# A graph kernel: the transposes of the adjacency matrix move from the attention scores into the first pass over reversed edges

## The reference, cut to what matters

```
x = layernorm(x + gcn3(x))            # three sums over incoming edges
x = layernorm(x + gat(x))             # per edge: a score from x_l[src], x_r[dst], weight; softmax by dst
x = layernorm(x + sage2(x))           # two sums over incoming edges
# the last layer sums over the REVERSED edges: out of a node, not into it
agg  = segment_sum(x[dst], src)       # row, col = src, dst
h    = relu(agg  / deg_out @ W1.T + b1)
agg2 = segment_sum(h[dst], src)
x = layernorm(x + relu(agg2 / deg_out @ W2.T + b2))
```

## Time and profile before

| | |
|---|---|
| median of three runs | 5697.41 us (5667.19 to 5700.05) |
| the profiled execution | 5702.34 us, of which its span is 5700.5 us |
| TensorE matmul busy | 3324.1 us, 58% |
| VectorE busy | 2808.7 us, 49% |
| ScalarE busy | 1675.3 us, 29% |
| GpSimd busy | 2048.7 us, 36% |
| scores stage | about 2350 to 3626 us |
| first back pass, strips | about 4954 to 5285 us |
| second back pass, strips | about 5308 to 5644 us |

### The profile page before, as it was taken

One profiled execution on the slowest core, in us unless ns is written; L12 is line 12 of the kernel. 1 busy time (PEld: TensorE's weight loads), 2 busy tenths in 40 slices (PEclk: granted clock), 3 DMA queues, 4 the chain that ended last, 5 costly groups with the idle time before them and its releaser, 6 DMA issues.

```text
span 5700.5 us, 61044 instructions
## 1 busy us (share of the span) xinstructions
PE 3324.1 (58%) x19159; PEld 3100.7 (54%) x19160; DVE 2808.7 (49%) x3801; ACT 1675.3 (29%) x2774; POOL 2048.7 (36%) x1982
## 2 busy tenths in 40 slices
PE   1300000019999999544444444357479999689697
PEld 0300000019999999544333343246379789589597
DVE  8300000024454544677666677788954344544345
ACT  0000000005645455200000000023266356456265
POOL 2777666750000000377677777346300000200300
PEclk9999999999999999755555555579789999799798
DMA  9700000008858587499899899247368268478585
GB/s 356 275 1 16 1 1 1 1 12 278 257 183 276 175 275 227 126 228 220 215 216 214 215 221 222 62 122 214 92 205 277 84 208 277 151 244 285 180 283 183
DMA packets 887483, 1008.44 MB, mean 177 GB/s; under 512 B 391651, under 2 KB 651705, under 8 KB 887270
## 3 DMA queue, kind: packets, MB, share of 16 engines
q1 hardware_dynamic: 795778, 861.50, 51.6%
q0 software_dynamic: 56208, 63.97, 4.8%
q10 hardware_dynamic: 35284, 80.30, 3.6%
HBM read 692.09 MB, written 233.14 MB: 162 GB/s over the span
## 4 chain that ended last, share of the span: by engine, by line
PE 44%; another core or an unknown queue 23%; DVE 14%; issue 11%; POOL 3%; ACT 2%; DMA 2%; DVEq 1%; SPq 0%; ACTq 0%; POOLq 0%
PE banks L918 35%; PE banks L841 4%; POOL work L624 2%; PE banks L1000 2%; DVE Z L1397 1%; DVE big L1519 1%; DVE Z L1402 1%; PE banks L863 1%; ACT banks L779 1%; DVE big L1406 1%; DMA work<-tab,stage 1%; DVE Z L1404 1%; ACT X L668 1%; PE banks L966 1%
## 5 line engine op out<-in xcount | busy, mean ns | idle before, releaser
L918 PE MATMUL banks<-wides,rows 128*128 128x384 f32 (+2 forms) x11040 | 2028.5, 344 | 155.8 <-issue 88.6
L918 PEld LDWEIGHTS banks<-wides,rows 128*128 128x128 f32 x11040 | 1949.4, 189 | 229.1 <-issue 94.3
L624 POOL DMA_INDIRECT work<-tab,stage x832 | 902.8, 1085 | 1483.0 <-ACT stage L771 1232.2
L1265 DVE CAST wides<-big 128x768 fp32r<-128x768 f16 (+3 forms) x1429 | 811.1, 569 | 1176.7 <-PE banks L918 1072.3
L698 ACT CAST wides<-big 128x768 fp32r<-128x768 f16 (+2 forms) x1037 | 832.2, 804 | 677.9 <-PE banks L918 554.3
L598 POOL DMA_INDIRECT cells<-queue_i x784 | 787.0, 1004 | 311.9 <-issue 298.6
L972 PE MATMUL banks<-V,work 128*128 x1664 | 372.5, 414 | 378.6 <-ACT work L773 312.1
L972 PEld LDWEIGHTS banks<-V,work 128*128 128x128 f32 x1664 | 345.1, 316 | 415.9 <-issue 415.9
L650 POOL DMA_INDIRECT V<-tab,nodei x100 | 96.2, 962 | 1201.9 <-DMA tab<-X 879.8
L863 PE MATMUL banks<-work 128*128 128x50 f16 x784 | 92.1, 278 | 670.6 <-issue 600.5
L863 PEld LDWEIGHTS banks<-work 128*128 128x128 f16 x784 | 73.1, 149 | 689.5 <-issue 612.6
(11 more groups left out here) (300 smaller groups left out, 3229.1 us busy)
## 6 DMA issues: line engine op xcount, KB each, us to landing
big<-cells SPq DMA_DIRECT2D x490, 416.0 KB
big<-cells SPq DMA_DIRECT2D x441, 384.0 KB
big<-turned SPq DMA_DIRECT2D x300, 384.0 KB
gathered<-work SPq DMA_DIRECT2D x104, 512.0 KB
work<-gathered SPq DMA_DIRECT2D x104, 512.0 KB, 4.2
big<-turned SPq DMA_DIRECT2D x100, 416.0 KB
cells<-work ACTq DMA_DIRECT2D x98, 416.0 KB, 14.6
turned<-big SPq DMA_DIRECT2D x50, 800.0 KB
```

Of the source, the lines that this page charges most:

```text
L624: pool.indirect_dma_start(msg[:, j, u, :], None, tab[0][:, :], bass.IndirectOffsetOnAxis(ap=stage[:, j * U + u:j * U + u + 1].bitcast(U32) ...
L918: last = pe.matmul(banks[:, 4 * (w % 2) + j, 0:(z - a) * P], rows2[:, s, part * D:(part + 1) * D], wides[:, q % QUEUE, (a - start) * P:(z ...
L1265: dve.tensor_copy(wides[:, (2 * m + 1) % QUEUE, 0:(z - a) * P], halves[:, m % HALVES, a * P:z * P]).then_inc(s_wided, 1)
```

## The change

The score loop loses its transposes and their saves: 26 rounds of gather stores remain. In the first back pass (`k == PASSES`) each strip is loaded by a DMA transpose of `adj` instead of a plain load of `turned`; two strips later SP waits until that strip has landed and stores it to `turned` (`keep`). A buffer is refilled only after its store has landed (`s_saved`, now one for each of the five buffers). The last two strips are stored after the loop, and SP waits for all stores before it loads for the second back pass, which is as before. POOL's and VectorE's waits on the saves become a wait on `s_kept_sum`, the store of `sumT`.

```diff
--- before.py
+++ after.py
@@ -184,8 +184,7 @@
         s_hi = sem("s_hi")
         s_hp = sem("s_hp")
         s_kept = sem("s_kept")
-        s_turn = [sem(f"s_turn{j}") for j in range(RING)]
-        s_saved = [sem(f"s_saved{j}") for j in range(RING)]
+        s_saved = [sem(f"s_saved{j}") for j in range(HALVES)]
         s_queue = [sem(f"s_queue{j}") for j in range(2)]
         s_xcol = [sem(f"s_xcol{j}") for j in range(8)]
         s_up = sem("s_up")
@@ -263,11 +262,6 @@
         OC = V
         qbuf = [work[:, WIDEN + j * QB:WIDEN + (j + 1) * QB].rearrange("p (a t n) -> p a t n", a=2, n=P) for j in range(2)]
         halves = big[:, HALFAT:HALFAT + HALVES * SWEEPS[0] * P // 2].bitcast(H16).rearrange("p (j c) -> p j c", j=HALVES)
-        PARTS = ((0, TILES // 2 + 1), (TILES // 2 + 1, TILES))
-        MOSTT = PARTS[0][1] * P
-        turns = big[:, 0:RING * MOSTT // 2].bitcast(H16).rearrange("p (j c) -> p j c", j=RING)
-        SAVED = 16 * (CT // 2) + 16
-        assert CT % 2 == 0 and CT // 2 <= ROUNDS and RING * MOSTT // 2 <= EXT0
         hidden = [big[:, 0:TW], big[:, TW:2 * TW]]
         hid = [a.rearrange("p (t f) -> p t f", f=D) for a in hidden]
 
@@ -471,6 +465,12 @@
             sp.wait_ge(s_go, go("cuts"))
             written = bounded(mybir.EngineType.SP, ready_i, 0, len(FIRST) - 1, PIECES)
 
+            def keep(k, q):
+                w, s = q // depth(k), q % depth(k)
+                m, tiles, c = strip_no(k, w, s), sweeps_of(k)[w], first_tile(k, w) * P
+                sp.wait_ge(s_half[m % HALVES], 16 * (m // HALVES + 1))
+                sp.dma_start(turned[s * P:(s + 1) * P, c:c + tiles * P], halves[:, m % HALVES, 0:tiles * P]).then_inc(s_saved[m % HALVES], 16)
+
             def dense_strips(k, first=0, last=None):
                 every = [(w, s) for w in range(len(sweeps_of(k))) for s in range(depth(k))]
                 for w, s in every[first:last]:
@@ -484,8 +484,17 @@
                     if m >= HALVES:
                         sp.wait_ge(s_widea, m - HALVES + 1)
                         sp.wait_ge(s_wided, m - HALVES + 1)
-                    matrix = turned if k in BACK else adj
-                    sp.dma_start(halves[:, m % HALVES, 0:tiles * P], matrix[s * P:(s + 1) * P, c:c + tiles * P]).then_inc(s_half[m % HALVES], 16)
+                    strip = halves[:, m % HALVES, 0:tiles * P]
+                    if k == PASSES:
+                        q = w * depth(k) + s
+                        if q >= HALVES:
+                            sp.wait_ge(s_saved[m % HALVES], 16 * (q // HALVES))
+                        sp.dma_start_transpose(strip.rearrange("p (o c) -> p o c", o=1), adj[c:c + tiles * P, s * P:(s + 1) * P]).then_inc(s_half[m % HALVES], 16)
+                        if q >= 2:
+                            keep(k, q - 2)
+                    else:
+                        matrix = turned if k in BACK else adj
+                        sp.dma_start(strip, matrix[s * P:(s + 1) * P, c:c + tiles * P]).then_inc(s_half[m % HALVES], 16)
 
             def rows_out(name, buf):
                 k = TABLES.index(name)
@@ -499,25 +508,7 @@
             rows_out("x_l", Z)
             sp.wait_ge(s_both, 1)
             sp.dma_start(ends_sum.rearrange("(t p) f -> p t f", p=P), sumT).then_inc(s_kept_sum, 16)
-            sp.wait_ge(s_kept_sum, 16)
-            for j in range(RING):
-                sp.sem_inc(s_saved[j], 16)
-
-            def save(i, j):
-                a, z = PARTS[j % 2]
-                sp.wait_ge(s_turn[j], i * 16 + 16)
-                sp.dma_start(turned[bass.ds(i * (2 * P) + j // 2 * P, P), a * P:z * P], turns[:, j, 0:(z - a) * P]).then_inc(s_saved[j], 16)
-
-            with sp.Fori(0, CT // 2) as i:
-                for j in range(RING):
-                    a, z = PARTS[j % 2]
-                    sp.wait_ge(s_saved[j], i * 16 + 16)
-                    sp.dma_start_transpose(turns[:, j, 0:(z - a) * P].rearrange("p (o c) -> p o c", o=1),
-                                           adj[a * P:z * P, bass.ds(i * (2 * P) + j // 2 * P, P)]).then_inc(s_turn[j], 16)
-                    sp.wait_ge(s_gath[j], i * (16 * U) + 16 * U)
-                    sp.dma_start(gathered[bass.ds(i * (RING * P) + j * P, P), :].rearrange("p (u f) -> p u f", u=U), msg[:, j, :, :]).then_inc(s_store[j], 16)
-                    save(i, j)
-            with sp.Fori(CT // 2, ROUNDS) as i:
+            with sp.Fori(0, ROUNDS) as i:
                 for j in range(RING):
                     sp.wait_ge(s_gath[j], i * (16 * U) + 16 * U)
                     sp.dma_start(gathered[bass.ds(i * (RING * P) + j * P, P), :].rearrange("p (u f) -> p u f", u=U), msg[:, j, :, :]).then_inc(s_store[j], 16)
@@ -539,12 +530,15 @@
             dense_strips(3)
             sp.wait_ge(s_pe, BATCH[f"q {NB - 1}"] + 1)
             dense_strips(4)
-            for j in range(RING):
-                sp.wait_ge(s_saved[j], SAVED)
             for r, (name, buf) in enumerate((("x3", X), ("h3", Z))):
                 dense_strips(PASSES + r, 0, HALVES)
                 rows_out(name, buf)
                 dense_strips(PASSES + r, HALVES)
+                if r == 0:
+                    for q in range(len(BACKS) * CT - 2, len(BACKS) * CT):
+                        keep(PASSES, q)
+                    for j in range(HALVES):
+                        sp.wait_ge(s_saved[j], 16 * (len(BACKS) * CT // HALVES))
             for n in range(NB):
                 sp.wait_ge(s_up, up("x4", n))
                 full = BT if n < NB - 1 else BT - 1
@@ -625,8 +619,7 @@
                                                 bass.IndirectOffsetOnAxis(ap=stage[:, j * U + u:j * U + u + 1].bitcast(U32), axis=0)).then_inc(s_gath[j], 16)
 
             pool.wait_ge(s_go, go("carried"))
-            for j in range(RING):
-                pool.wait_ge(s_saved[j], SAVED)
+            pool.wait_ge(s_kept_sum, 16)
             pool.memset(accP, 0.0).then_inc(s_blank, 1)
             pool.wait_ge(s_exp, 1)
             with pool.Fori(0, ROUNDS) as i:
@@ -1434,8 +1427,7 @@
             for h in range(H):
                 evac(f"rows of scores {h}", scores_rows(h))
             flat = lambda a: a.rearrange("p g e -> p (g e)")
-            for j in range(RING):
-                dve.wait_ge(s_saved[j], SAVED)
+            dve.wait_ge(s_kept_sum, 16)
             for c in range(C5):
                 link(dve.tensor_tensor_scan(flat(F5[:, c, :, :]), flat(penF), flat(A5[:, c, :, :]), -BIG, ALU.add, ALU.max))
                 link(dve.tensor_tensor_scan(flat(A5[:, c, :, :])[:, ::-1], flat(penB)[:, ::-1], flat(F5[:, c, :, :])[:, ::-1], -BIG, ALU.add, ALU.max))

```

## The result

The changed kernel takes 5889 us (median of four, 5863 to 5917) against 5697: ratio 1.0335, interval 1.0296 to 1.0373. The profiled execution took 5917.21 us, 214.9 more than that of before.

| stage | before | after | difference |
|---|---|---|---|
| to the first matmul of the dense passes | 1274.2 | 1319.0 | +44.8 |
| from there to the first gather of the scores | 1076.2 | 1076.1 | -0.1 |
| gathers of the scores, first to last | 1272.3 | 1251.4 | -20.9 |
| to the first strip of the first back pass | 1332.0 | 1326.0 | -6.0 |
| first back pass, first to last matmul | 330.8 | 529.3 | +198.5 |

A forecast was written before the change was run, and what follows sets the result against it. POOL's issue was taken to bound the scores and PE the first back pass, with DMA binding that pass after the change: 5702 + 365 + 3 - 10 = 6060, or 6055 as median; range 6000 to 6120, 8 in 10 5950 to 6170.

The forecast's parts named there:

- the price of a strip: First back pass: transpose plus store take 3.3 us a strip instead of 1.41, adding 365 us over 193 strips.
- lower bound: First back pass: load and store each at 282 GB/s, 2.85 us a strip, +278 us.
- a sign of being wrong: First back pass: a step per strip under 2.8 us or over 3.8 us would show the forecast wrong.
- upper bound: First back pass: 3.8 us a strip, from the scores' DMA shares with and without transposes and saves; +461 us.
- The value between: First back pass: 1.5 and 1.9 us from windows behind a save and a transpose, 3.4 together; 3.3 taken.
- My working with that figure: First back pass: transpose load at 261 GB/s, 1.54 us, plus 1.4 for the store: 2.94 us a strip, +295 us.
- the gain there: Scores: removing transposes and saves ends no wait of POOL; 10 us gained, bounds 0 and 110 us.
- late releases by PE: Scores: while POOL issues without pause, PE's release sometimes comes late and POOL runs dry; not the transposes' doing; 120 us.
- Rivals 1: Scores: late releases come from loaded DMA engines and vanish, -110 us instead of -10, total 5955; chance 0.10.
- 2: Rival, scores: DMA is the bound, so freeing it gives 333 us back, total 5640, faster; chance 0.03.
- 3: Rival, first back pass: stores and transposes hinder each other, 3.8 to 4.1 us a strip, total 6150 to 6210; chance 0.10.
- 4: Rival, scores: lighter DMA lets POOL pause less, late releases come oftener, +100 us, total 6160; chance 0.05.

The follow-up runs named there:

- e5: Changed kernel with each first-back-pass strip loaded plainly twice, nothing stored, second back pass on plain strips of adj: 1.93 us a strip.
- e8: Changed kernel with each first-back-pass strip transposed twice, nothing stored, second back pass on plain strips of adj: 4.01 us a strip.
- e7: Changed kernel with each strip stored twice, the second time to a spare tensor: 3.44 us a strip.
- a0: The changed kernel itself, run again on another chip: 5365 against 5166 us, ratio 1.0387, 2.45 us a strip.
- e2: Changed kernel without the stores of the strips, second back pass on plain strips of adj: 5273 us, ratio 1.0205, 1.99 us a strip.
- b0: The kernel before, unchanged, on a chip without the late releases: 5162 us, gathers of the scores 1143.5 us.
- e1: Kernel before without the scores' transposes and saves, both back passes on plain strips of adj: 5159.5 against 5163.1 us, ratio 0.9996.
- e12: Kernel before without the scores' transposes and saves, on a chip with late releases: 5698 against 5713 us, ratio 0.9983.
- x2: Kernel before with GpSimd waiting for each batch of seven gathers in both back passes, chip with late releases: 5642 against 5713 us, ratio 0.988.

## Why the prediction was wrong

**The step that failed** is the price of a strip, 3.3 us with a lower bound of 2.85; measured 2.45, under the 2.8 that I had named as a sign of being wrong. The path was right, the size wasn't. The lower bound said "load and store each at the plain load's rate of this pass, 282 GB/s". That rate was PE's demand, not what the DMA engines can do: PE was 100% busy, took a strip each 1.41 us, and the transfers kept up. e5 shows 415 GB/s, 1.0 us for a strip and not 1.42. I had read the share of 0.88 as "an eighth left"; the share goes to 1.18 in the changed kernel and 1.22 in e8, so it is no measure of room. My upper bound of 3.8 counted on the same shares and fell with them.

**The value between** read 1.5 us for a store and 1.9 for a transpose from single windows and added them. Each part was off in its own way: a store costs 1.0 us of shared time (e7 against a0: 3.44 - 2.45), and the transpose's 1.9, which e2 bears out at 1.99, is a limit of its own, of which only 1.45 counts beside other transfers, so 0.55 us of a store is hidden. Both windows were of stretches in which SyncE waited for each transpose before the next. With the measured step the working gives 193 x (2.45 - 1.41) = 201 us; the trace shows 198.5. The total would then be 5891, near the median of 5889. That it comes so near is luck in part: the profiles show 27 us won before the pass where I had 10, and 45 us of the first stretch that aren't the change's.

**The page's figure.** The Trainium skill, "DMA: Bandwidth & Descriptors", "Latency and other measured facts", has 261 GB/s for a transpose with a non-contiguous middle dimension; alone, this one made 201 (e2), and the measurement decides. My working with that figure (+295) was too high because it added 1.4 us for the store.

**Right:** the direction and the cause; that POOL's issue sets the scores and the full DMA engines there were beside it (b0 against e1, share 0.99 against 0.34, same pace); the gain there, 10 us forecast, 21 in the profile and 0 to 22 in e12; that late releases by PE don't need the transposes (they stay in e12, if a little fewer) and that, at the start of the back passes, they go away when GpSimd pauses (x2); the second back pass unchanged, 1.41 us a strip; the waits of `keep`, hidden. Rivals 1, 2, 3 and 4 are all out: the scores neither gained 110 us nor lost any, and the step was not 3.8.

**Also wrong:** the granted clock. I expected about 0.55 with PE 43% busy; PE was 70% busy at 0.98. It made no odds for the sum. In e8 PE is 56% busy at 0.76.

## What to carry to other kernels

A transfer rate or a DMA share read where another engine is the bound is a demand, not a capacity; it can't be a lower bound of what more transfers cost. Where a stage is bound by an engine's own issue, DMA work beside it can be nearly free even at a share of 0.9 to 1.0 (0 to 20 us of 1270 here), and moving it to a stage bound by TensorE with plain loads already under way can make it cost (+200 us here). When two transfers are overlapped, price them as the larger of each one's own limit and the sum of their shared parts, and measure both with one kernel that doubles a part.

## What the runs showed of the hardware that was not expected

- The two limits fitted to the table above: 2.0 us of its own and 1.45 us shared for a transpose of 0.4 MB, 1.0 us for a plain transfer of the same size in either direction.
- The DMA share of a window reads up to 1.22 with transposes, and 1.03 at 415 GB/s without them.
- The same kernel took 5163 to 5166 us on three chips and 5697 to 5713 on others. In the slower profiles VectorE and ScalarE stand in waits, of some 21 us each in the loop of column counts, that the profile calls "remote", while GpSimd issues indirect DMAs with hardly a pause; in the profiles of the faster chips there is no such wait, though GpSimd issues at the same pace. In the loop of column counts the code lets VectorE wait for PE alone. PE's matmuls there end at 707.98 us, and VectorE goes on at 728.41, 20.4 us later:

```profile
707.03 0.95 PE L863 MATMUL banks<-work 128*128 128x50 f16 x8 [21.44 <-issue]
```

What differs between the chips isn't known.
